# The last product of a graph convolution: W3 held still instead of h2, its result transposed by TensorE

## What is computed

```python
def _slconv(x, adj, S, W):                # called with S = adj, so the weighting is adj * adj
    return einsum('nm,bmh->bnh', adj * S, einsum('bnf,fh->bnh', x, W))
h = relu(_slconv(x, adj, adj, W1))        # 128 -> 256
h = relu(_slconv(h, adj, adj, W2))        # 256 -> 512
x = layernorm(x + _slconv(h, adj, adj, W3))   # 512 -> 128
```

## Time and profile before

| what | value |
|---|---|
| median of three runs | 1156.65 us |
| lowest and highest run | 1156.28 and 1158.54 us |
| span of the profiled execution | 1154.9 us |
| TensorE busy (matmul) | 1121.8 us, 97% of the span |
| VectorE busy | 583.2 us, 50% |
| ScalarE busy | 386.3 us, 33% |
| mean granted TensorE clock | 0.989 of full |
| first block, four pairs | from about 23 us to 540 us |

### The profile page before, as it was taken

How to read it: one execution, slowest core, us unless ns; L and a number is a source line. 1 busy time by engine, 2 the same in 40 slices (tenths; PEclk the granted TensorE clock), 3 DMA queues, 4 the chain that set the end, 5 groups by cost and what they waited for, 6 DMA issues and landing times.

```text
span 1154.9 us, 15131 instructions
## 1 busy us (share of the span) xinstructions
PE 1121.8 (97%) x5688; PEld 937.5 (81%) x5688; DVE 583.2 (50%) x1426; ACT 386.3 (33%) x696; POOL 0.7 (0%) x6
## 2 busy tenths in 40 slices
PE   6999999999999999999999999999999999999994
PEld 4888988899888988888776878878788787778694
DVE  7233364243442264247646545565655646565667
ACT  6222012120222012133424443444434443435442
POOL 0000000000000000000000000000000000000000
PEclk9999999999999999999999999999999999999997
DMA  9200000000000000012000000000000000000001
GB/s 312 85 1 1 1 1 1 1 1 1 0 0 0 0 0 0 0 39 106 1 1 1 1 1 1 1 19 1 19 1 0 18 0 2 17 19 1 1 19 37
DMA packets 21744, 20.43 MB, mean 18 GB/s; under 512 B 960, under 2 KB 18496, under 8 KB 21696
## 3 DMA queue, kind: packets, MB, share of 16 engines
q1 hardware_dynamic: 21696, 19.81, 5.4%
HBM read 15.61 MB, written 4.19 MB: 17 GB/s over the span
## 4 chain that ended last, share of the span: by engine, by line
PE 94%; DVE 3%; ACT 1%; DMA 0%; issue 0%; ACTq 0%; SPq 0%; DVEq 0%
PE ps L464 27%; PE ps L465 27%; PE ps L466 27%; PE ps L584 8%; PE ps L563 4%; PE ps L566 1%; DVE adj L916 1%; PE ps L755 1%; PE ps L754 0%; DMA xb<-in_x 0%; PE ps L600 0%; DVE square L982 0%; DVE stats L933 0%; DVE node L916 0%; DVE xb L974 0%
## 5 line engine op out<-in xcount | busy, mean ns | idle before, releaser
L861 ACT ACTIVATE gates<-ps,lb 128x256 f32<-128x256 f32 (+2 forms) x273 | 142.6, 567 | 168.1 <-PE ps L466 155.1
L464 PE MATMUL ps<-adj,node 128*128 128x512 f32 x384 | 151.9, 396 | 12.8 <-DVE adj L916 10.1
L465 PE MATMUL ps<-adj,node 128*128 128x512 f32 x384 | 150.3, 391 | 0.0
L466 PE MATMUL ps<-adj,node 128*128 128x512 f32 x384 | 150.3, 391 | 0.0
L801 ACT ACTIVATE y<-ps 128x512 fp32r<-128x512 f32 x48 | 28.7, 598 | 294.5 <-PE ps L466 294.4
L916 DVE TENSOR_TENSOR y<-ps,y 128x512 fp32r<-128x512 f32 x48 | 33.1, 691 | 186.0 <-ACT y L801 186.0
L466 PE MATMUL ps<-ht,lw 128*128 128x256 f32 (+2 forms) x231 | 112.1, 485 | 0.0
L465 PE MATMUL ps<-ht,lw 128*128 128x256 f32 (+2 forms) x231 | 111.9, 485 | 0.0
L464 PE MATMUL ps<-ht,lw 128*128 128x256 f32 (+2 forms) x231 | 111.0, 480 | 0.0
L464 PE MATMUL ps<-adj,h 128*128 128x512 f32 x256 | 99.7, 389 | 0.0
L465 PE MATMUL ps<-adj,h 128*128 128x512 f32 x256 | 99.7, 389 | 0.0
(11 more groups left out here) (167 smaller groups left out, 1975.5 us busy)
## 6 DMA issues: line engine op xcount, KB each, us to landing
square<-in_adj_t SPq DMA_DIRECT2D x8, 512.0 KB, 8.0
xb<-in_x SPq DMA_DIRECT2D x8, 512.0 KB, 7.5
adj_raw<-in_adj_t SPq DMA_DIRECT2D x8, 512.0 KB, 7.7
out<-xb SPq DMA_DIRECT2D x7, 512.0 KB, 3.2
lw_raw<-in_wih_t SPq DMA_DIRECT2D x1, 1024.0 KB, 5.8
lw_raw<-in_whh_t SPq DMA_DIRECT2D x1, 768.0 KB, 7.3
w_raw<-in_w SPq DMA_DIRECT2D x1, 512.0 KB, 11.0
out<-xb SPq DMA_DIRECT2D x2, 256.0 KB, 2.5
```

Source lines behind the costliest of these rows:

```text
L464: pe.matmul(dst, stat(HI), mov(HI), start=start, stop=False)
L465: pe.matmul(dst, stat(HI), mov(LO), start=False, stop=False)
L466: return pe.matmul(dst, stat(LO), mov(HI), start=False, stop=stop)
L861: nc.scalar.activation(gates_in(u.stream)[:, g, at], ps[:, (AHEAD["gate"][slot] + gate) % GB, 0:u.n], ACT.Tanh if g == GG else ACT.Sigmoid ...
```

## The change

P3 is done the other way round. W3's 128x128 blocks are the held operand and h2 streams with 512 columns, one unit of 12 matmuls for each half of the nodes (S3_UNIT); the three terms add up in PSUM, so the cross term has no place of its own. The result has features on the partitions. VectorE copies it to SBUF as plain float32 (`s3t`, 128x1024, in the space of y2), and TensorE turns it in four 128x128 float32 blocks for each half (`turn_half`, unit TURNED, a matmul in transpose mode against the identity `ident_f`). From the turned unit ScalarE writes s3's HI part and VectorE its LO part, straight from PSUM. `cross` and `s3full` are gone.

The units stand in a new order, the table TAIL_UNITS: h2 half 0 (4 units), h2 half 1 g = 0 and 1, product of half 0, h2 half 1 g = 2 and 3, turn half 0, product of half 1, turn half 1. In the second batch of a pair the turn of half 1 is put behind the first tile (m = 0) of A3. Its number q still counts among the units ahead of A3. TensorE waits once more at the start, for the identity, and the line that used to overwrite `ident_f` with ones is gone.

The core of the diff:

```diff
+        s3t = sb("s3t", [P, N], F32, r2_at)
...
-        cross = sb("cross", [P, 2, 2, F], F32, cross_at)
...
-        s3full = sb("s3full", [P, 2, F], F32)
...
-        A1, P1, A2, P2, P3, A3 = HALVES, MT * H1 // BANK, HALVES * K2, HALVES * K3, MT // 2, MT // 2
+        A1, P1, A2, P2, P3, A3 = HALVES, MT * H1 // BANK, HALVES * K2, HALVES * K3, 2 * HALVES, MT // 2
         A_MM = A1 + P1 + A2 + P2 + P3
         A_LO = A_MM + 1
         A_MM_PAIR, A_LO_PAIR = 2 * A_MM + A3, 2 * A_LO + A3
-        A_HI_PAIR = 2 * A_LO
+        A_HI = A_LO - HALVES
+        A_HI_PAIR = 2 * A_HI
         A_PRE = 1 + MT + 2
         W1_AT = 5
+        H2_UNIT, S3_UNIT, TURNED = 0, 1, 2
+        TAIL_UNITS = ([(H2_UNIT, 0, g) for g in range(K3)] + [(H2_UNIT, 1, 0), (H2_UNIT, 1, 1), (S3_UNIT, 0, 0), (H2_UNIT, 1, 2), (H2_UNIT, 1, 3),
+                      (TURNED, 0, 0), (S3_UNIT, 1, 0), (TURNED, 1, 0)])
+        assert K3 == 4 and len(TAIL_UNITS) == P2 + P3
+        def tail_unit(j, *unit):
+            return j * A_MM + A1 + P1 + A2 + TAIL_UNITS.index(unit)
...
-                    for half in range(HALVES):
-                        lo_reached(a_lo_of(y2_unit + (half + 1) * K2 - 1))
-                        for g in range(K3):
+                    def turn_half(half):
+                        q = tail_unit(j, TURNED, half, 0)
+                        bank_free(q)
+                        lo_reached(a_lo_of(tail_unit(j, S3_UNIT, half, 0)))
+                        for t in range(4):
+                            nt = (4 * half + t) * P
+                            last = pe.transpose(ps[:, q % BANKS, t * F:(t + 1) * F], s3t[:, nt:nt + P], ident_f[:])
+                        last.then_inc(a_mm, 1)
+                    for what, half, g in TAIL_UNITS:
+                        cols = slice(half * BANK, (half + 1) * BANK)
+                        if what == H2_UNIT:
                             bank_free(q)
+                            lo_reached(a_lo_of(y2_unit + (half + 1) * K2 - 1))
                             for k in range(K2):
                                 last = product(ps[:, q % BANKS, :], lambda i: w2s[:, i, k, g * P:(g + 1) * P],
-                                               lambda i: y2[:, i, k, half * BANK:(half + 1) * BANK],
-                                               k == 0, k == K2 - 1)
+                                               lambda i: y2[:, i, k, cols], k == 0, k == K2 - 1)
                             last.then_inc(a_mm, 1)
-                            q += 1
-                    h2_unit = y2_unit + A2
-                    for u in range(P3):
-                        bank_free(q)
-                        half = u * 2 * P // BANK
-                        lo_reached(a_lo_of(h2_unit + (half + 1) * K3 - 1))
-                        for t in range(2):
-                            nt = (2 * u + t) * P
+                        elif what == S3_UNIT:
+                            bank_free(q)
+                            lo_reached(a_lo_of(tail_unit(j, H2_UNIT, half, K3 - 1)))
                             for k in range(K3):
-                                pe.matmul(ps[:, q % BANKS, 2 * t * F:(2 * t + 2) * F], h2[:, HI, k, nt:nt + P],
-                                          w3s[:, k, :, :].rearrange("p a c -> p (a c)"),
-                                          start=(k == 0), stop=False, skip_group_check=True)
-                                last = pe.matmul(ps[:, q % BANKS, 2 * t * F:(2 * t + 1) * F],
-                                                 h2[:, LO, k, nt:nt + P], w3s[:, k, HI, :],
-                                                 start=False, stop=(k == K3 - 1), skip_group_check=True)
-                        last.then_inc(a_mm, 1)
+                                last = product(ps[:, q % BANKS, :], lambda i: w3s[:, k, i, :],
+                                               lambda i: h2[:, i, k, cols], k == 0, k == K3 - 1)
+                            last.then_inc(a_mm, 1)
+                        elif (j, half) != (1, 1):
+                            turn_half(half)
                         q += 1
                 for m in range(MT):
-                    lo_reached(a_lo_of(2 * A_MM - A3 + m // 2))
+                    if m == 1:
+                        turn_half(1)
+                    lo_reached(a_lo_of(tail_unit(1, TURNED, m // 4, 0)))
                     for u in range(A3):
                         if m == 0:
                             bank_free(q + u)
...
                     if m < MT - 1:
                         last.then_inc(adj_used, 1)
+            pe.wait_ge(eye_set, 2)
             pair_products(0, first=True)
             with pe.Fori(1, PAIRS) as it:
                 pair_products(it)
...
                     act.wait_ge(xr_in, 16 * (B - 1))
                     x_hi((it * 2 + (j + 1)) % B, a_hi)
-                    for half in range(HALVES):
-                        for g in range(K3):
-                            hi_part(h2[:, HI, g, half * BANK:(half + 1) * BANK], ACT.Relu)
-                            q += 1
-                    for u in range(P3):
-                        act.wait_ge(a_mm, mm0 + (q + 1))
-                        if u >= 2:
-                            act.wait_ge(a_lo, it * A_LO_PAIR + (A_PRE + a_lo_of(j * A_MM + q - 2)))
-                        nc.scalar.activation(
-                            cross[:, u % 2], ps[:, (j * A_MM + q) % BANKS, :].rearrange(
-                                "p (t a c) -> p t a c", t=2, a=2)[:, :, 1, :], ACT.Copy).then_inc(a_hi, 1)
+                    for what, half, g in TAIL_UNITS:
+                        cols = slice(half * BANK, (half + 1) * BANK)
+                        if what == H2_UNIT:
+                            hi_part(h2[:, HI, g, cols], ACT.Relu)
+                        elif what == TURNED:
+                            act.wait_ge(a_mm, mm0 + (q + 1))
+                            nc.scalar.activation(
+                                s3[:, HI, 4 * half:4 * half + 4, j, :], ps[:, (j * A_MM + q) % BANKS, :].rearrange(
+                                    "p (t c) -> p t c", t=4), ACT.Copy).then_inc(a_hi, 1)
...
                     hi_ready()
                     x_lo((it * 2 + (j + 1)) % B, a_lo)
                     n_hi += 1
-                    for half in range(HALVES):
-                        for g in range(K3):
+                    for what, half, g in TAIL_UNITS:
+                        cols = slice(half * BANK, (half + 1) * BANK)
+                        if what == H2_UNIT:
                             hi_ready()
-                            cols = slice(half * BANK, (half + 1) * BANK)
                             lo_relu(h2[:, LO, g, cols], bank(), h2[:, HI, g, cols], a_lo)
-                            q, n_hi = q + 1, n_hi + 1
-                    for u in range(P3):
-                        own_at = own0 + (j * 2 * P3 + 2 * u)
-                        hi_ready()
-                        if u > 0:
-                            dve.wait_ge(a_lo, it * A_LO_PAIR + (A_PRE + a_lo_of(j * A_MM + q - 1)))
-                        nc.vector.tensor_tensor(
-                            s3full[:], bank().rearrange("p (t a c) -> p t a c", t=2, a=2)[:, :, 0, :],
-                            cross[:, u % 2], ALU.add).then_inc(own, 1)
-                        dve.wait_ge(own, own_at + 1)
-                        nc.vector.tensor_copy(s3[:, HI, 2 * u:2 * u + 2, j, :], s3full[:]).then_inc(own, 1)
-                        dve.wait_ge(own, own_at + 2)
-                        lo_part(s3[:, LO, 2 * u:2 * u + 2, j, :], s3full[:],
-                                s3[:, HI, 2 * u:2 * u + 2, j, :], a_lo)
+                        elif what == S3_UNIT:
+                            dve.wait_ge(a_mm, it * A_MM_PAIR + (j * A_MM + q + 1))
+                            nc.vector.tensor_copy(s3t[:, cols], bank()).then_inc(a_lo, 1)
+                            n_hi -= 1
+                        else:
+                            hi_ready()
+                            hi = s3[:, HI, 4 * half:4 * half + 4, j, :]
+                            lo_part(s3[:, LO, 4 * half:4 * half + 4, j, :], bank().rearrange("p (t c) -> p t c", t=4),
+                                    hi, a_lo)
...
-            nc.vector.memset(ident_f[:], 1.0).then_inc(own, 1)
-            dve.wait_ge(own, A_OWN + 5)
-            nc.vector.tensor_copy(ones[:], ident_f[:]).then_inc(const_set, 1)
-            own_pre = 5
+            dve.wait_ge(own, 4)
+            nc.vector.memset(f32(ones[:]), 1.0).then_inc(const_set, 1)
```

More of the change, by code:

```diff
@@ L1001, in _ @@
                     w3s[:, :, HI, :], a_lo)
-            A_OWN = 2 * (2 * P3)
             def pair(it, first=False):
-                own0 = it * A_OWN + own_pre
                 if not first:
@@ L1011, in pair @@
                 for j in range(2):
-                    hi0 = it * A_HI_PAIR + (A_PRE + j * A_LO)
+                    hi0 = it * A_HI_PAIR + (A_PRE + j * A_HI)
                     q = 0
@@ L1084, in pair_stats @@
```

(16 more changed lines are left out.)

## The result

The changed kernel takes 1163.59 us (median of four runs, 1163.01 to 1165.35) against 1157.31 us for the kernel before (four runs, 1156.28 to 1158.54). The medians are 6.3 us or 0.54% apart, where 8.7 us had been forecast. The ratio of the runs on record is 1.0067, with a 95% interval of 1.0055 to 1.0079, which would be 7.7 us. How it is formed is not on record, so the size is known as 6 to 8 us, and that the kernel is slower is clear. The profiled execution took 1163.81 us, with a span of 1162.0 us against 1154.9 before, 7.1 us more. Two of the 13 runs of the kernel before that stand beside the first group of experiments took 1350 and 1509 us at a mean granted clock of 0.75 and 0.65, and are left out of that group's median and ratios.

A forecast was written before the change was run, and what follows sets the result against it. TensorE, busy 97% of the span, was taken as the bound. Loop -8.1 + 9.8 + 3.8 = +5.5 us, handover +1.45, clock +1.7 gave +8.7 us, so 1165.4 us; range 1159.5 to 1175.

The forecast's parts named there:

- Removed and added work: TensorE's stream: P3 removed, 58.8 us; reversed product 43.5 and 64 transposes 7.15 added; gain 8.1 us.
- rival of four passes: Transposes: float32 blocks take four passes, 21.4 us more, 1186.8 us; chance 0.07.
- cheap end for transposes: Part of rival "cheap ends" (1159.7 us, chance 0.08): transposes at 0.06 us each, -3.3 us.
- The wait ahead of the product: Before half 1's product, TensorE waits for the last h2 unit's LO part: 1.23 us a batch, 9.8 in all.
- The wait ahead of the turn: Before half 1's turn, TensorE waits for VectorE's copy: 0.96 us in each pair's first batch, 3.8 in all.
- The handover: Into the second block: SP's loads start 3.3 us later against A3, VectorE bounds, TensorE's gap about 2.8 us; +1.45 us.
- The clock behind the handover: After the 2.8 us handover gap the granted clock falls to 0.5; 1.7 us lost, ends 0 and 3.3.
- The sum: Whole kernel: 5.5 + 1.45 + 1.7 = +8.7 us, median 1165.4 us; chance 0.65.
- The clock in the loop: Rival: clock falls within the batches, +6.8 us (1172.2) in first batches or +13.6 (1179.0) in all eight; chance 0.15.
- Hidden waits: Rival: TensorE finds both results ready ahead of product and turn; -5.0 us, 1151.7 us; chance 0.05.

The follow-up runs named there:

- the first group of experiments: One of two groups in which seven follow-up kernels were run, each beside the kernel before on the same chip (medians 1155.86 and 1155.69 us).
- Turn 0 twice: Changed kernel with each of the 32 transposes of half 0 issued twice; 1163.12 us, ratio 1.0054 to the kernel before.
- Products behind all of h2: Changed kernel with units reordered: all eight h2 units, product of half 0, product of half 1, turn 0, turn 1; 1159.09 us, ratio 1.0017.
- turn 1 twice: Changed kernel with each of the 32 transposes of half 1 issued twice; 1167.63 us, ratio 1.0102 to the kernel before.
- both waits covered: Changed kernel reordered: h2, product 0, turn 0 inside product 1, turn 1 inside the next batch's A1 or behind A3's first tile; 1151.65 us, ratio 0.9961.
- last turn later: Changed kernel with the last turn behind two tiles of A3 instead of one; 1168.32 us, ratio 1.0104 to the kernel before.
- loads by the copy: Changed kernel with SP's loads of the plain matrix waiting for VectorE's copy of the last product, not the last turn; 1161.93 us, ratio 1.0045.
- both covered, loads by the copy: Changed kernel with covered-waits order and SP waiting for VectorE's copy of the last product; 1149.35 us, ratio 0.9947 to the kernel before.

## Why the prediction was right, and where it was off

**Removed and added work: right.** Forecast 58.8 - 43.5 - 7.15. A product of one half takes 2.72 us, twice that is the forecast 5.44. The transposes cost 0.109 us each, where 0.112 was taken. The variant with covered waits shows the gain of 8.1 us on the path. The rival of four passes is ruled out, and the cheap end for transposes too.

**The wait ahead of the product: right.** Forecast 1.57 + 0.11 - 0.45; found 1.57 and 0.11, and 0.44 for the transposes. That the engines do the same on the same shapes behind h2 as behind y1 is what made this work; the row of y1 was there in the trace of before because a wait of 0.1 us had made it visible. Turn 0 twice shows that the wait, not the transposes, is the price.

**The wait ahead of the turn: right, the copy mis-sized.** I took 0.60 us for a one-input pass from PSUM, ScalarE's figure; VectorE takes 0.69, the same as with two inputs. That is 0.4 us over the four pairs. Forecast per pair +1.39, found +1.40. That it agrees so closely is partly luck: the longer copy is set off by the 0.11 us for the load ahead of the first transpose, which did not show.

**The handover: the mechanism right, the size off in the profiled run.** The step that failed is "+1.45 us". It took the landing time of the second tile from one execution, 7.4 us after SP's first issue. In the profiles of all nine kernels it is 6.2 to 7.5 us, and the changed kernel's profile had the shortest, 6.2. There the restart of TensorE stood at 25.1 us behind A3's start, where I expected 26.4 and before had 24.5. Turn 0 twice has the same handover and a landing of 7.2 us, and it restarts 26.1 us behind A3: +1.2 net of the turn. "Products behind all of h2", with the longest landing, restarts 26.7 us behind A3: +1.5 net of the turn and of 0.27 us of A3's own wait. So the term is 0.2 to 1.5 us, as the landing falls.

The clock in the last column is that of the stretch right at the restart:

| kernel | SP's first issue behind A3's start, us | second tile landed after that, us | TensorE's gap, us | clock at 0.5 for, us |
|---|---|---|---|---|
| before | 0.03 | 7.37 | 1.39 | 0 |
| the change | 3.34 | 6.22 | 1.66 | 0 |
| turn 1 twice | 3.78 | 6.75 | 2.20 | 0 |
| turn 0 twice | 3.34 | 7.22 | 2.66 | 3.4 |
| both waits covered | 3.61 | 7.25 | 2.70 | 6.8 |
| products behind all of h2 | 3.61 | 7.51 | 2.97 | 3.4 |
| last turn later | 6.21 | 7.24 | 5.55 | 6.8 |
| loads by the copy | 0.76 | 7.17 | 1.39 | 0 |
| both covered, loads by the copy | 0.74 | 6.83 | 1.39 | 0 |

In the five kernels whose loads wait for the turn behind one tile of A3 (rows two to six) the gap is the landing less 4.54 to 4.56 us. So VectorE's chain from the second tile on is the bound there, as the prediction had it, and with a landing of 7.37 us this relation gives the forecast gap, 2.8 us. Only the landing was not to be read from one execution.

**The clock behind the handover: not in the profiled run, but in others.** The step was "2.8 us is longer than either, so I expect a fall". The gap was 1.66 us, and the clock stayed. Four variants with gaps of 2.66 us or more show the fall, so a gap of 2.8 us would very likely have brought it. But the comparison "longer than either" (1.97 us and 2.15 us of standing in the earlier trace rows) is not the rule: in turn 1 twice TensorE stood 2.20 us, longer than both, and the clock stayed. The length of the low stretch isn't set by the gap either, 3.4 us behind 2.66 and 6.8 behind 2.70.

**The sum: close partly by luck.** The span's 7.1 us are made up of 5.6 in the pairs (forecast 5.5), 0.5 at the start, where the first A3 came that much later than the pair's own terms give, 0.2 at the handover (forecast 1.45, and 1.7 for the clock), and 0.8 in the second block (615.7 us from TensorE's restart to the end, 614.9 before). Nobody forecast the 0.5 and the 0.8, and they make up for 1.3 of the 3.0 us by which the handover and the clock came out short. Both look like scatter: the first A3 starts at 122.9 to 123.4 us in the changed kernel and in the three variants with the same path up to there (turn 0 twice, loads by the copy, last turn later), and from restart to end the nine profiles take 613.0 to 616.8 us, falls of the clock behind the handover included.

**The clock in the loop: the rival fell.** 0.45 us of transposes and 1.1 us of standing, eight times, left the granted clock at 1.00 from 30 to 530 us, in every stretch of 10 us. The Trainium skill ("TensorE: Matmul & The Clock Gate", Part 4, PE-mode transpose) says that the full clock doesn't engage for transposes. Here they came in groups of four or eight within dense matmuls, and the clock did not fall, so for this use the measurement decides against the rule; a long run of nothing but transposes was not tried.

**Hidden waits: wrong for this change, and the way out of it.** That rival needed waits under 0.6 us a batch. The order of the change doesn't give that; another order does, and then the kernel is faster.

**Left open.** How much the earlier loads save in the median (0.2% and 0.1% by the ratios, with overlapping intervals, both in the same direction); why the landing of the second tile varies by 1.3 us; what decides on the clock between 2.20 and 2.66 us of standing, and on the length of its fall.

## What to carry to other kernels

A change that makes the busiest engine's work cheaper must keep its cover: for each result that this engine hands out and gets back through others, measure the round trip once in the old trace (here 1.57 us), and ask of the new order what stands between. The same instructions gave +0.67% or -0.39%, by order alone, and -0.53% once the loads of the matrix waited for the copy instead of the turn. A step moved past a unit also moves whatever waits for the unit's number, here a DMA queue that had 1.4 us to spare; and a term that rests on one DMA's landing deserves a range, since it scattered by 1.3 us.

## What the runs showed of the hardware

A float32 block of 128x128 in transpose mode costs TensorE as much as a 128-column float32r matmul with its own held operand, about 0.11 us. The load of such a block is recorded shorter than a float32r load, 141 ns against about 190, and the pace is the same (line L540 of the changed kernel, min/median/max ns):

```profile
L540 PEld LDWEIGHTS ps<-ident_f,s3t x64: 137/141/143, 63.3 to 524.1; 128*128 128x128 f32 x64
```

VectorE's plain copy of 512 float32 columns from PSUM takes as long as a pass with two inputs, 0.69 us:

```profile
L1043 DVE COPY s3t<-ps x16: 691/692/693, 61.0 to 521.2; 128x512 f32<-128x512 f32 x16
```

The granted clock fell at each of the four handover gaps of 2.66 us or more and at none of the five of 2.20 us or less. In two of the four it was down before TensorE went on: with both waits covered at 533.5 us, 0.8 us ahead of the restart, and with the last turn later at 547.0, 2.9 us ahead.
